# One array shape for a causal attention phase, with paired score blocks and held scatters

## The reference, cut to what matters

```python
q, k, v = (h @ W.T).reshape(b, L, 16, 16)          # b=2, L=2048, 16 heads of 16
scores = einsum('bnhd,bmhd->bhnm', q, k) / 4.0     # causal
att_t = softmax(scores inside the own and the previous 64-token segment)
out_t = einsum('bhnm,bmhd->bhnd', att_t, v)
att = softmax(scores)                              # all earlier tokens
pcs = (att * exp(index_decays)).sum over the 64 rows of a segment      # 32 x 2048
w = decayed sum of pcs over earlier segments, normalised
kv = einsum('bhrs,bshd,bshe->brhde', w, k, v)      # 32 x 16 x 16 per head
out_lin = einsum('brlhd,brhde->bhrle', q, kv)
y = sigmoid(mix) * out_t + (1 - sigmoid(mix)) * out_lin
```

## Time and profile before

| what | value |
|---|---|
| median of 3 runs | 2689.44 us (2684.31 to 2692.98) |
| time of the profiled execution | 2683.82 us |
| its span (first to last instruction) | 2682.1 us |
| mean granted TensorE clock | 0.92 |
| busy over the span: PE, DVE, ACT, POOL | 85%, 69%, 58%, 57% |

### The profile page before, as it was taken

One profiled execution on the slowest core, in us unless ns is written; L12 is line 12 of the kernel. 1 busy time (PEld: TensorE's weight loads), 2 busy tenths in 40 slices (PEclk: granted clock), 3 DMA queues, 4 the chain that ended last, 5 costly groups with the idle time before them and its releaser, 6 DMA issues. The chain is left out here.

```text
span 2682.1 us, 79472 instructions
## 1 busy us (share of the span) xinstructions
PE 2271.7 (85%) x30000; PEld 1484.3 (55%) x30000; DVE 1851.7 (69%) x4635; ACT 1556.0 (58%) x3824; POOL 1530.2 (57%) x3168
## 2 busy tenths in 40 slices
PE   8799999999999999998759934489999998786793
PEld 5445555555555555546538823366776766664583
DVE  6578888888888888874445564277777776573456
ACT  5577777777777777772323321366666665553231
POOL 3357777777777777778545546444554444255452
PEclk9889999999999999999789955699999998887897
DMA  6911111111121111103437562201111111642456
GB/s 216 265 31 39 39 38 38 39 38 39 38 66 39 38 39 39 38 21 119 158 107 230 177 217 107 96 22 51 51 51 51 51 39 35 222 155 75 147 151 228
DMA packets 188728, 243.87 MB, mean 91 GB/s; under 512 B 41672, under 2 KB 144981, under 8 KB 187456
## 3 DMA queue, kind: packets, MB, share of 16 engines
q1 hardware_dynamic: 161824, 182.08, 22.5%
q0 software_dynamic: 19872, 50.41, 5.4%
q10 hardware_dynamic: 6656, 6.31, 0.7%
HBM read 136.08 MB, written 106.50 MB: 90 GB/s over the span
## 5 line engine op out<-in xcount | busy, mean ns | idle before, releaser
L724 DVE TENSOR_REDUCE at_mn<-at_S 128x1 f32<-128x1024 f32 (+4 forms) x704 | 612.2, 880 | 156.7 <-PE at_S L823 152.2
L658 ACT ACTIVATE at_E<-at_S,at_mn 128x1024 f32<-128x1024 f32 (+4 forms) x704 | 596.4, 848 | 202.6 <-DVE at_mn L724 200.8
L865 PE MATMUL at_pcs<-at_E,at_c 128*32 128x256 f32 (+1 forms) x4864 | 435.0, 347 | 0.0
L823 PE MATMUL at_S<-am_sk,am_sq 96*128 96x512 bf16 (+3 forms) x1152 | 334.2, 354 | 28.1 <-ACT at_E L658 23.2
L597 POOL TENSOR_TENSOR at_kvo<-am_kh,am_vh 128x256 f32<-128x256 f32 x512 | 303.7, 627 | 0.0
L1332 POOL DMA_INDIRECT expert_out<-m_ysb,m_dst x158 | 155.4, 983 | 143.2 <-issue 76.2
L865 PEld LDWEIGHTS at_pcs<-at_E,at_c 128*32 128x32 f32 x4864 | 186.8, 109 | 87.2 <-issue 81.6
L582 POOL TENSOR_TENSOR at_half<-at_half 128x128 f32<-128x128 f32 (+4 forms) x640 | 185.3, 290 | 50.1
L865 PE MATMUL at_pcs<-at_Tt,at_c 128*32 128x128 f32 x1024 | 209.7, 287 | 0.0
L648 ACT ACTIVATE at_Tt<-at_S,at_mn 128x192 f32<-128x192 f32 x512 | 173.4, 426 | 45.9 <-DVE at_mn L714 45.8
L823 PEld LDWEIGHTS at_S<-am_sk,am_sq 96*128 96x128 bf16 x1152 | 78.5, 97 | 203.6 <-issue 116.0
(11 more groups left out here) (392 smaller groups left out, 5530.1 us busy)
## 6 DMA issues: line engine op xcount, KB each, us to landing
m_xg<-expert_rows SPq DMA_DIRECT2D x158, 129.0 KB
am_sq<-q_parts SPq DMA_DIRECT2D x192, 64.0 KB, 2.3
am_sk<-k_parts SPq DMA_DIRECT2D x192, 64.0 KB, 2.2
memory_rows<-m_blank SPq DMA_DIRECT2D x16, 516.0 KB
gl_hx<-memory_rows SPq DMA_DIRECT2D x32, 258.0 KB, 3.4
m_wgu<-in_f_wgu SPq DMA_DIRECT2D x2, 4096.0 KB
rt_yin<-expert_out SPq DMA_DIRECT2D x7, 1024.0 KB, 11.9
fn_yin<-expert_out SPq DMA_DIRECT2D x7, 1024.0 KB, 8.5
```

The source lines that it names most:

```text
L658: nc.scalar.activation(E[:, at:at + w], S[v % NS_B][:, 0:w], ACT.Exp, bias=mn[:, q, s, 1 + j:2 + j], scale=-1.0, accum_out=rs[:, q, s, 1 + ...
L724: nc.vector.tensor_reduce(mn[:, q, s, 1 + j:2 + j], S[v % NS_B][:, 0:w], AX.X, ALU.min).then_inc(s_mn, 1)
L823: ins = nc.tensor.matmul(S[v % NS_B][:, c:c + cw], sq[:, u, t * P:(t + 1) * P], sk[:, u, c0 + c:c0 + c + cw], start=True, stop=True)
L865: ins = nc.tensor.matmul(pcs[j * R:(j + 1) * R, cols[0]:cols[1]].rearrange("p (b c) -> p b c", c=P), lhsT, rhs, start=(n, j) not in touche ...
```

## The change

1. **One array shape.** Each product of the attention phase that had 128 or 64 columns of weights is cut into four (`STRIPS`), each with 32 columns of weights into 32 output rows: the mask and score products of `window`, `scores`, `values`, `turn_pcs`.
2. **Turning by products.** The `transposes` calls become one call, `turned`: 4 tiles x 2 halves x 4 strips of ordinary f32 products with a part of the unit matrix, 64 columns each. `turn_pcs` becomes 16 such products of 128 columns.
3. **Paired blocks.** Two blocks of a group that have the same width of at most 512 share one buffer and one reduction on VectorE (two results); ScalarE still takes an exponential for each. The groups then have 4, 5, 5 and 4 blocks, pairs last.
4. **New order on TensorE**, below. `products` is cut in halves: one at the end of loop 2, one in loop 3 behind the window. ScalarE's `keep_kvr` moves from behind the fifth block of loop 2 to behind the window's exponentials of loop 3.
5. **Held scatters.** Before the scatters of step n the three passes wait until all scatters of the steps before have landed.

```diff
+        STRIPS = [slice(x, x + R) for x in range(0, P, R)]
+        def blocks(q):
+            every = [(s, j, c0, w) for s, t in enumerate(QUADS[q]) for j, (c0, w) in enumerate(chunks(t))]
+            small = [[b for b in every if b[3] == w] for w in sorted({b[3] for b in every if b[3] <= CW})]
+            paired = [pair for pair in small if len(pair) == 2]
+            alone = [[b] for b in every if not any(b in pair for pair in paired)]
+            return alone + paired
...
                 if g + 1 < NG:
                     window_exps(g + 1)
+                    if n and q == 3:
+                        keep_kvr(n - 1)
...
-                        if n and k == 5 and q == 2:
-                            keep_kvr(n - 1)
...
+                        for x in STRIPS:
+                            ins = nc.tensor.matmul(S[v % NS_B][x, at:at + cw], sq[:, u, t * P + x.start:t * P + x.stop],
+                                                   sk[:, u, c0 + c:c0 + c + cw], start=True, stop=True)
...
-                    ins = nc.tensor.transpose(M[:, s * P + e * SEG:s * P + (e + 1) * SEG],
-                                              Tt[half, q, s, e * SEG:e * SEG + P], ident[half, half])
+                    for e in range(2):
+                        for x in STRIPS:
+                            ins = nc.tensor.matmul(M[x, s * P + e * SEG:s * P + (e + 1) * SEG],
+                                                   Tt[:, q, s, e * SEG + x.start:e * SEG + x.stop],
+                                                   ident[:, e * SEG:(e + 1) * SEG], start=True, stop=True)
...
                 if g + 1 < NG:
                     window(g + 1)
+                if n and q == 3:
+                    products(n - 1, 1)
                 next_sums(g, 0, (0, 1))
                 next_scores(g, 1)
-                transposes(g, 0)
+                turned(g)
+                next_scores(g, 2)
                 next_sums(g, 1, (0, 1))
-                next_scores(g, 2)
-                transposes(g, 1)
                 next_sums(g, 2, (0,))
                 next_scores(g, 3)
+                values(g)
                 next_sums(g, 2, (1,))
-                values(g)
                 next_scores(g, 4)
-                next_sums(g, 3, (0,))
+                next_sums(g, 3, (0, 1))
                 next_scores(g, 5)
-                next_sums(g, 3, (1,))
                 if n and q == 1:
                     turn_pcs(n - 1)
                 if n and q == 2:
-                    products(n - 1)
+                    products(n - 1, 0)
                 if n and q == 3:
                     decayed(n - 1)
-                next_scores(g, 6)
...
+                if n:
+                    pool.wait_ge(sent, n * G * TOPK * 16)
```

More of the change, by code:

```diff
@@ L802, in window @@
                 for b in range(2):
[L803 to L804 removed]
+                    for x in STRIPS:
+                        nc.tensor.matmul(S[v % NS_B][x, b * CW:b * CW + 2 * TW], identb[:, x],
+                                         mask[:, 1 if q == 0 and b == 0 else 0, :], start=True, stop=True)
                     for s in range(2 * b, 2 * b + 2):
@@ L825, in scores, with turned @@
                 ins.then_inc(s_S, 1)
-            def transposes(g, e):
+            def turned(g):
                 q = g % NQ
[L829 to L841, removed]
-                for s in range(NQ):
-                    ins = nc.tensor.transpose(M[:, s * P + e * SEG:s * P + (e + 1) * SEG],
-                                              Tt[half, q, s, e * SEG:e * SEG + P], ident[half, half])
+                pe.wait_ge(s_E, unit(g, 0) + 1)
+                if g:
+                    pe.wait_ge(s_Y, g)
+                if g >= NQ and q == 2:
+                    pe.wait_ge(s_pTs, g // NQ)
+                if g >= NQ and q == 3:
+                    pe.wait_ge(s_kvr, g // NQ)
+                if g >= 2 * NQ and q == 0:
+                    pe.wait_ge(s_kvn, g // NQ - 1)
+                for s in range(NQ):
+                    for e in range(2):
+                        for x in STRIPS:
+                            ins = nc.tensor.matmul(M[x, s * P + e * SEG:s * P + (e + 1) * SEG],
+                                                   Tt[:, q, s, e * SEG + x.start:e * SEG + x.stop],
+                                                   ident[:, e * SEG:(e + 1) * SEG], start=True, stop=True)
@@ L898, in turn_pcs, with products @@
                 for j in range(4):
-                    ins = nc.tensor.transpose(M[:, j * P:(j + 1) * P], pcs_s[:, j * P:(j + 1) * P], ident[:, :])
+                    for x in STRIPS:
+                        ins = nc.tensor.matmul(M[x, j * P:(j + 1) * P], pcs_s[:, j * P + x.start:j * P + x.stop], ident[:, :],
+                                               start=True, stop=True)
                 ins.then_inc(s_pT, 1)
-            def products(n):
-                pe.wait_ge(s_pTs, n + 1)
-                pe.wait_ge(s_kvo, n + 1)
-                pe.wait_ge(s_Y, min(n * NQ + NQ + 3, NG))
-                for t in range(NT):
+            def products(n, part):
+                if part == 0:
+                    pe.wait_ge(s_pTs, n + 1)
+                    pe.wait_ge(s_kvo, n + 1)
+                    pe.wait_ge(s_Y, min(n * NQ + NQ + 3, NG))
+                for t in range(part * NT // 2, (part + 1) * NT // 2):
                     j = t % 4
@@ L956, in _ @@
             turn_pcs(NHEAD - 1)
-            products(NHEAD - 1)
+            products(NHEAD - 1, 0)
+            products(NHEAD - 1, 1)
             decayed(NHEAD - 1)
```

56 lines of the change are left out of this document (35 added, 21 removed).

## The result

The changed kernel takes 2683.88 us (median of 12 runs, 2669.08 to 2691.60), the kernel before beside it 2691.74 us (12 runs, 2684.31 to 2698.46): ratio 0.996, 95% interval 0.9945 to 0.9976. I had forecast 2670. The profiled execution has a span of 2683.3 us and took 2684.99.

A forecast was written before the change was run, and what follows sets the result against it. TensorE was late most, around a ring of three buffers, with no engine far below. Loops summed to 32.85 against 33.41 us a head, -18 us for 32 heads, other parts zero: 2670 us, range 2605 to 2720.

The forecast's parts named there:

- From below nothing, since no transfer becomes shorter by the hold: Held scatters in three passes: lower end of the holds' cost, nothing; the term taken was zero, 42 us at most.
- VectorE's slots cover it: Held scatters: GpSimd waits 2.13 us for VectorE's slots anyway at a pass's last hold, so holds cost zero.
- loop 1: Attention: from 8.13 to 8.0 us, 7.4 by TensorE's work plus about 0.6 standing for the copy that `values` needs.
- loop 0: Attention: from 8.05 to 6.8 us, less 15 shape changes of 0.09, plus 0.3 for `turned`, less 0.15 for `values`.
- the wait on M in loop 3: `turned` needs bank M, read by `keep_kvr`; second block late, VectorE waits 1.8 us; loop 3 goes to 9.95.
- pairs at zero: Paired blocks on VectorE: four reductions fewer save about 0.1 us each; nothing in the sum, at most 13 us.
- C: Rival, loop 3: the hold on bank M costs more; 33.8 us a head, +11 us or more, 2700; chance 0.26.
- B: Rival, loop 3: the hold on bank M costs less, loop stays near 7.6 to 8 us; 2600; chance 0.20.
- D: Rival, window and score products: bf16 strips move at the f32 rate, 8.8 us a head; about 2910; chance 0.04.
- E: Rival, attention: 96-row and 128-row products are different shapes, so switches stay; head 38 us, 2830; chance 0.03.
- F: Rival, `turned` and `values`: short strips start at twice the 14 ns spacing, 115 us more, 2785; chance 0.03.
- GpSimd at zero: Attention: GpSimd's inverse comes 0.3 to 0.5 us late for `outputs`, hidden by VectorE's slack; uncovered, 0.5 x 2 a head.

The follow-up runs named there:

- kvr_mid_free: The changed kernel without the holds, with `keep_kvr` ahead of the window's exponentials of loop 3, products still divided: 2573.56 us, ratio 0.9904 to the kernel before.
- pcs_early: kvr_mid_free with `keep_pcs` behind the third exponentials of loop 0 instead of the fourth: 2560.03 us, ratio 0.9826 to the kernel before.
- shapes_only: The kernel before with every attention product in strips, in the old order, without pairs or holds: 2567.06 us, ratio 0.9864.
- unpaired: The changed kernel, holds included, with each small block in a buffer of its own: 2660.40 us, ratio 1.0219 to the kernel before.
- pcs_tt_early: pcs_early with `keep_transposed` behind VectorE's first minima of a loop instead of the second: 2549.05 us, ratio 0.9779 to the kernel before.

## Why the prediction was wrong

It said 18 us less in attention and nothing from the scatters; on the first chip it was 17 more and some 25 less. Two errors of opposite sign left the total near, by luck: 8 us less where I had said some 20. Both terms failed, and each has its own step.

**The step that failed in the scatters: "From below nothing, since no transfer becomes shorter by the hold".** The term of zero and its lower end left out that the phases can get shorter though no transfer does. On chips of the first kind a hold gains (0.9889 by itself); 0.9889 times 1.006 is 0.9948, beside 0.996 (0.9945 to 0.9976) measured. On other chips the same step failed the other way: "VectorE's slots cover it" was read from one wait, 2.13 us in the earlier trace rows. That wait was itself late by the stalls. Where nothing stalls the slots of the last step are 11 us ahead and each hold costs its landing of 2 us; the bound of 42 us, worked out for a hold without cover, is what was measured (43). The trace of before had the sign: waits of GpSimd for slots of 8.07 us in a chain of engines of which none was busy. The forecast gave no term to them.

**The loops: the step that failed in attention is loop 1, "8.0".** Measured against forecast: loop 0 7.06 (6.8), loop 1 8.72 (8.0), loop 2 8.23 (8.1), loop 3 9.82 (9.95), together 33.83 (32.85); the mean over all heads, four of them with a drop of the clock, is 34.0. So the mechanism that I put in the middle, the wait on M in loop 3, was right in place and size, and kvr_mid_free, which moves the copy alone beside leaving the holds out, shows that it is the cause: 1.4 us a head come back. The term mis-sized is loop 1, 0.7 us of the 1.0 that were missing. I followed `values` and its copy there and not the first sums, which need `keep_pcs`. That copy stands behind the fourth exponentials as before, but the pairs, put last, moved larger blocks ahead of it: it starts 7.54 us behind loop 0's window, against 6.34 without pairs, and TensorE waits 1.4 us for it. pcs_early, with the pairs kept, gives 0.44 us of loop 1 back.

**Loop 0 came near by luck.** I took 1.25 us off it, nearly all for changes of shape that fall away. shapes_only and unpaired have all those changes away and a loop 0 of 8.08 and 8.06 us, as long as before. The 1.0 us came with the pairs, which I had priced at nothing, and they took 0.9 back in loop 1. So what the shapes gave lies in the other loops, and "pairs at zero" is right for a head and wrong for each of the two loops. Which property of the pairs shortens loop 0, fewer units or their order, was not tested.

**Rivals.** C (the hold on M costs more, 33.8 us a head) has the right length of head, but not its mechanism: loop 3 was as forecast, and the loss came from loop 1. B fell. D fell: a set of bf16 strips takes 0.22 us, no more than the whole product. E fell: the switches are gone, and shapes_only gives their worth, 35 us, against the 5.1 - 0.95 = 4.15 us a head, 133 us in all, that TensorE saved by my sum; I had said that this is not the gain. F fell: rows of `turned` start 14 ns apart and those of `values` 0.26/31 = 8 ns. The rule of 25 ns between starts (the Trainium skill, TensorE: Matmul & The Clock Gate, Part 1) does not hold in this trace for rows of 17 and 64 columns on a quarter of the array.

**The rest.** Pairs at zero: right in the sum (unpaired, 3 us at most). GpSimd at zero: VectorE waits 6.6 us in 800 for the inverse's sum, 0.3 us a time; right. "An expert pass longer by more than 1 us" as a sign of error: they were shorter on the first chip and 15 to 19 us longer with the hold on the others. So this sign did not catch the step on the first chip.

**Open.** What ScalarE and VectorE wait for in the stalls on such chips, and what makes these chips different; chip against occasion is told apart only in so far as one chip took 2601 and 2603 us on two occasions, while each reading of 2690 us stands alone. Shown is that the stalls are there with the unbroken rows of scatters, shrink with pauses between them and don't need table loads. That they end with the row of scatters is read from the traces, not tested: GpSimd waits for the stalled engines too, so which of the two ends the other is not told apart. pcs_tt_early wasn't run on such a chip, with the hold or without. What sets off the drops of the clock is open too: pcs_early has none in the middle of the phase, but shapes_only has four and pcs_tt_early three without any wait for `keep_pcs`.

## What to carry to other kernels

Before an edit that frees an engine, list for each stretch what the engine will reach earlier and which copies of other engines must then be earlier too: here attention was 17 us longer than before with two copies of 0.4 and 0.6 us on ScalarE where the change had put them, 44 us shorter with both moved, and 57 with one on VectorE moved as well. A place counted in instructions ("behind the fourth") moves when the order of the instructions does: pairs priced at nothing shifted a microsecond from one loop to the next. And a loop whose length comes out as forecast is not yet a mechanism shown. Unexplained idle time of several engines at once in the trace of before is a term with two signs, not cover. And where a change touches DMA traffic, time it on more than one chip before calling it good.

## What the runs showed of the hardware that I had not expected

- The same kernel takes 2600 us on three chips and 2690 on two occasions elsewhere, with attention equal within 0.1% (1094.9 and 1094.5 us); of the 81 us between the two profiled executions 71 are in the three phases that scatter, 10 in `gl`. A wait for landed scatters is worth +1.7% on the one kind and -1.1% on the other.
- TensorE's granted clock falls to 0.51 (the lower level, 1.2 GHz) from 622.4 to 625.8 in a phase in which it is otherwise 1.00, just behind the 1.4 us for which TensorE stood for `keep_pcs`; so in four heads of the changed kernel, each 1.4 to 1.8 us longer for it. That wait is not needed: in shapes_only three of the four drops from 200 to 1150 us follow a wait of 0.82 us for exponentials. In the kernel before, with TensorE busy 97%, there is no drop in that stretch and every head from the third on takes 33.4 to 33.5 us.
- Most changes of array shape show as an idle time of up to 0.4 us of the weight loads, charged to nothing: 226.9 us in 800 for the three groups L865, L823 and L843 of before (720 times, 0.32 each; that is 30 a head, which has 57 changes).
- Four strips of 32 weight columns move bf16 columns as fast as one product of 128: 0.22 us for a set of 512 columns (0.44 for two), where a whole product took 0.23.
